# Masking the weighted values of two tiles in one VectorE instruction

## The reference, cut to what matters

```
x = x + conv(_gn(x), W)
q, k, v = qkv[0] * SCALE, qkv[1], qkv[2]          # 16 heads of 8
logits[a, b] = einsum(q, k shifted by (a, b)) + rpb[a, b]     # 49 neighbours
attn = softmax(logits)
out = sum over (a, b) of attn[a, b] * (v shifted by (a, b))
x = x + (out @ w_proj + b_proj)
```

## Time and profile before

| | |
|---|---|
| median of 3 runs | 1097.95 us (1097.91 to 1101.18) |
| profiled execution | 1098.98 us |
| its span, first to last instruction | 1097.2 us |
| mean granted TensorE clock | 0.95 |
| busy: PE, DVE, ACT, POOL | 988.8, 810.7, 642.0, 484.6 us |
| `select_heads` on DVE (L1174) | 512 instructions, 128.1 us |
| attention, 32 chunks | from about 260 us to 1065 us |

### The profile page before, as it was taken

How to read it: one execution, slowest core, us unless ns; L and a number is a source line. 1 busy time by engine, 2 the same in 40 slices (tenths; PEclk the granted TensorE clock), 3 DMA queues, 4 the chain that set the end, 5 groups by cost and what they waited for, 6 DMA issues and landing times.

```text
span 1097.2 us, 41269 instructions
## 1 busy us (share of the span) xinstructions
PE 988.8 (90%) x16485; PEld 684.8 (62%) x16485; DVE 810.7 (74%) x2111; ACT 642.0 (59%) x1808; POOL 484.6 (44%) x839
## 2 busy tenths in 40 slices
PE   4999999998999989899998999898999999999882
PEld 3666665564676666666676666666666666666651
DVE  3387774544888787879888888978798788878760
ACT  2111124003786868587877767785868677777561
POOL 5000103203654646374646556474756464555530
PEclk9999999998999989899999999998999899999895
DMA  9321002234467555555746576655657375646311
GB/s 254 91 89 45 31 16 104 92 87 147 131 159 212 150 162 157 161 164 152 218 119 196 145 206 168 166 165 161 173 138 221 95 214 136 204 114 195 97 48 57
DMA packets 122582, 154.73 MB, mean 141 GB/s; under 512 B 30832, under 2 KB 107024, under 8 KB 119064
## 3 DMA queue, kind: packets, MB, share of 16 engines
q1 hardware_dynamic: 121112, 148.20, 48.1%
q0 software_dynamic: 992, 3.90, 1.2%
q10 hardware_dynamic: 288, 0.00, 0.0%
HBM read 84.05 MB, written 67.60 MB: 138 GB/s over the span
## 4 chain that ended last, share of the span: by engine, by line
PE 68%; DVE 10%; ACT 9%; issue 8%; DMA 3%; ACTq 1%; SPq 1%; POOL 0%; POOLq 0%; DVEq 0%
PE PS L1313 16%; PE PS L1380 13%; PE PS L1419 10%; PE PS L1403 8%; PE PS L1325 6%; PE PS L1396 6%; PE PS L1362 5%; ACT area L805 3%; DVE area L1142 3%; DVE S L1163 3%; ACT S L897 3%; DVE masked L1174 2%; PE PS L1342 2%; DMA bqkv<-b_qkv 2%; PE PS L1429 1%
## 5 line engine op out<-in xcount | busy, mean ns | idle before, releaser
L687 POOL TENSOR_TENSOR late<-masked 128x48 f32<-128x48 f32 (+1 forms) x512 | 153.3, 300 | 368.3 <-DVE masked L1174 356.1
L897 ACT ACTIVATE S<-S 128x384 f32<-128x384 f32 (+1 forms) x512 | 283.0, 555 | 24.1 <-DVE S L1163 21.1
L1163 DVE TENSOR_TENSOR S<-PS,bias 128x384 f32<-128x384 f32 (+1 forms) x512 | 282.5, 552 | 2.9 <-PE PS L1380 0.2
L1380 PE MATMUL PS<-area 97*128 97x48 bf16 (+1 forms) x4096 | 249.9, 207 | 36.4 <-DVE S L1163 32.8
L1153 DVE TENSOR_REDUCE mcol<-PS 128x6 bf16<-128x480 f32 (+2 forms) x288 | 176.1, 612 | 124.5 <-PE PS L1403 124.4
L890 ACT ACTIVATE VT<-PS 128x128 f32<-128x128 f32 x448 | 132.5, 296 | 183.5 <-PE PS L1362 179.5
L1380 PEld LDWEIGHTS PS<-area 97*128 97x128 bf16 x4096 | 178.6, 102 | 83.1 <-DVE S L1163 41.3
L1419 PE MATMUL PS<-S,VT 128*18 128x48 f32 x8192 | 196.4, 214 | 12.1 <-issue 11.5
L1313 PE MATMUL PS<-padded,wconv 128*128 128x392 f32 x576 | 204.2, 503 | 3.3 <-DVE wconv L1199 3.3
L1419 PEld LDWEIGHTS PS<-S,VT 128*18 128x18 f32 x8192 | 117.1, 99 | 135.3 <-issue 69.5
L1403 PEld LDWEIGHTS PS<-area 128*128 128x128 bf16 x1568 | 144.9, 156 | 22.2 <-issue 7.4
(11 more groups left out here) (86 smaller groups left out, 921.4 us busy)
## 6 DMA issues: line engine op xcount, KB each, us to landing
area<-k_parts SPq DMA_DIRECT2D x32, 1008.0 KB, 7.1
area<-q_parts SPq DMA_DIRECT2D x64, 294.0 KB, 8.2
k_parts<-area SPq DMA_DIRECT2D x32, 504.0 KB, 8.1
k_parts<-area SPq DMA_DIRECT2D x32, 336.0 KB, 3.0
q_parts<-area SPq DMA_DIRECT2D x32, 294.0 KB, 6.7
late<-x_mid SPq DMA_DIRECT2D x18, 392.0 KB, 4.9
out<-area SPq DMA_DIRECT2D x18, 392.0 KB, 4.1
den<-sums SPq DMA_DIRECT2D x132, 49.0 KB
```

The source lines that it names most:

```text
L687: nc.gpsimd.tensor_tensor(sel[:, c % SEL_RING, :, :, t0:t0 + count], m[:, :, 0], m[:, :, 1], ALU.add).then_inc(s["summed"], 1)
L897: nc.scalar.activation(S[:, n % 4, 0:cols], S[:, n % 4, 0:cols], ACT.Exp).then_inc(s["probs"], 1)
L1163: nc.vector.tensor_tensor(S[:, n % 4, 0:cols], PS[:, SCORE + n % 2, 0:cols], bias[:, at:at + cols], ALU.add).then_inc(s["biased"], 1)
L1380: last = mm(PS[:, SCORE + n % 2, cols * g:cols * (g + 1)], key_rows[a][0:PEAK_ROW + 1, g, key:key + 128], query_rows[a][0:PEAK_ROW + 1, :, ...
```

## The change

`masked` grows from 2 x 128 to 2 x 256 columns and PE puts the weighted values of tiles 2P and 2P + 1 side by side into one bank, SUM + P % 2. `select_heads` is called in odd steps only, for the pair of tiles n - 3 and n - 2, and does one instruction over both (two where the tiles have different numbers of patches, tiles 14 and 15). It waits until both tiles are weighted. `weigh` of a tile of pair P waits until pair P - 2 is selected. POOL's instructions and their order stay as they are, but tile 2P is now signalled by the instruction that also signals tile 2P + 1.

```diff
+        def pair_offset(c, n):
+            return GROUPS * PATCH * tile_of(c % 2, n - 1)[1] // 2 if n % 2 else 0
...
-                m = masked[:, n % 2, 0:4 * q].rearrange("p (g h a t) -> p g h a t", g=2, h=GROUP_HEADS, a=PATCH)
+                first = pair_offset(c, n)
+                m = masked[:, T // 2 % 2, first:first + 4 * q].rearrange("p (g h a t) -> p g h a t", g=2, h=GROUP_HEADS, a=PATCH)
...
-                wait(dve, "weighted", T + 1)
-                wait(dve, "summed", T - 1)
...
+                pair = (TILES * c + n) // 2
+                wait(dve, "weighted", 2 * pair + 2)
+                if pair > 1:
+                    wait(dve, "summed", 2 * (pair - 1))
+                at, cols = 0, [GROUPS * PATCH * tile_of(c % 2, m)[1] // 2 for m in (n, n + 1)]
+                for size, tiles in [(2 * cols[0], 2)] if cols[0] == cols[1] else [(cols[0], 1), (cols[1], 1)]:
+                    src, to = (p.rearrange("p (g h q) -> p g h q", g=2 * tiles, h=GROUP_HEADS) for p in (
+                        PS[:, SUM + pair % 2, at:at + size], masked[:, pair % 2, at:at + size]))
+                    mask = cst[:, C_OUT:C_OUT + GROUP_HEADS].unsqueeze(1).unsqueeze(3).broadcast_to(list(src.shape))
+                    nc.vector.tensor_tensor(to, src, mask, ALU.mult).then_inc(s["selected"], tiles)
+                    at += size
...
-                    if n > 1 or c:
-                        select_heads(*next_tile(c, n, -2))
+                    if n % 2 and (n > 1 or c):
+                        select_heads(*next_tile(c, n, -3))
...
-                wait(pe, "selected", T - 1)
+                pair, first = T // 2, pair_offset(c, n)
+                if pair > 1:
+                    wait(pe, "selected", 2 * (pair - 1))
```

More of the change, by code:

```diff
@@ L255, in build @@
         mcol = sb("mcol", [128, PATCHES], BF16)
-        masked = sb("masked", [128, 2, 128])
+        masked = sb("masked", [128, 2, 256])
         halves = sb("halves", [128, 2, 128])
@@ L1166, in select_heads @@
             def select_heads(c, n):
-                q = PATCH * tile_of(c % 2, n)[1]
-                T = TILES * c + n
-                wait(dve, "weighted", T + 1)
-                wait(dve, "summed", T - 1)
-                src = PS[:, SUM + n % 2, 0:4 * q].rearrange("p (g h q) -> p g h q", g=2, h=GROUP_HEADS)
-                mask = cst[:, C_OUT:C_OUT + GROUP_HEADS].unsqueeze(1).unsqueeze(3).broadcast_to([128, 2, GROUP_HEADS, q])
-                nc.vector.tensor_tensor(masked[:, n % 2, 0:4 * q].rearrange("p (g h q) -> p g h q", g=2, h=GROUP_HEADS), src, mask,
-                                        ALU.mult).then_inc(s["selected"], 1)
+                pair = (TILES * c + n) // 2
[9 more added lines that the diff above has]
+                    at += size
             def invert(c):
@@ L1261, in _ @@
                         divide(c)
-            for n in range(TILES - 2, TILES):
-                select_heads(CHUNKS - 1, n)
+            select_heads(CHUNKS - 1, TILES - 2)
             divide(2 * IMAGES)
@@ L1415, in weigh @@
                     wait(pe, "value_out", w + 1)
-                wait(pe, "selected", T - 1)
+                pair, first = T // 2, pair_offset(c, n)
+                if pair > 1:
+                    wait(pe, "selected", 2 * (pair - 1))
                 for g in range(GROUPS):
-                    at = q * (g // 4)
-                    last = mm(PS[32 * (g % 4):32 * (g % 4) + VALUE_COLS, SUM + n % 2, at:at + q], VT[:, w % 4, g, :],
+                    at = first + q * (g // 4)
+                    last = mm(PS[32 * (g % 4):32 * (g % 4) + VALUE_COLS, SUM + pair % 2, at:at + q], VT[:, w % 4, g, :],
                               S[:, n % 4, q * g:q * (g + 1)], start=True, stop=True)
```

## The result

The changed kernel took 1125.95 us (median of 4 runs, 1124.85 to 1128.57) and the kernel before, in runs beside it, 1097.93. The ratio is 1.0263, with a 95% interval from 1.0236 to 1.0290. The forecast was 1117 us and the range ended at 1124: the sign was right, the size was not. The profiled execution took 1128.57 us, with a span of 1126.0, so 29.6 us more than the profiled one of before (1098.98).

What follows compares the result with a forecast made beforehand. The prediction took PE to bound the kernel (68% of the chain), with DVE setting the pace at the end of even chunks. Its terms, 10.5 + 8 + 0.3 = +19 us on 1097.95, gave 1117 us, range 1095 to 1124.

Steps and rivals of the forecast that it cites:

- Part 1: DVE's masked product at the end of even chunks: over a pair it occupies 0.26 us, saving 0.37 us per even chunk.
- Part 2: End of even chunks: POOL's bunched subtractions hold DVE's spreads, PE waits 0.70 us longer, 15 times, +10.5 us.
- Part 3: Odd chunks: POOL's pieces of Qbd start later, the first held by divide; PE waits about 0.6 us, +8 us in all.
- Part 4: Small effects: POOL's last two adds at the very end run one behind the other, +0.3 us; later stores count 0.
- Sum: Whole kernel: 10.5 + 8 + 0.3 = +19 us on the median of 1097.95, giving 1117 us.
- slower still: Rival: later stores and loads, or PE's longer idle times bringing more low clock, give 1125 us and over; chance 0.08.

Runs made afterwards that it cites:

- e9: Changed kernel with e8's POOL order, POOL's second subtraction cut to 8 columns from the second image on, so output incomplete: ratio 0.9702.
- e10: Kernel before, one product per tile, with e8's POOL order and POOL's second subtraction cut to 8 columns from the second image on: ratio 0.9757.
- e1: Kernel before, single products, but POOL waits until both tiles of a pair are selected and masked has four places: 1120.36 us.
- e4: Changed kernel, POOL's order in even steps made subtraction (from step 8), piece of Qbd, then add: 1094.27 us.
- e5: Kernel before, one product per tile, with the POOL order of e4: ratio 0.9980.
- e2: Changed kernel, but in even steps of odd chunks POOL writes its piece of Qbd before adding the heads: 1104.88 us.
- e6: Changed kernel plus two unused 480-column matmuls on PE ahead of the scores in steps 12 to 16: ratio 1.0156.
- e12: e8 with the extra PE matmuls of e6 in steps 12 to 16: 1086.81 us.
- e8: e4 with the last two first-kind subtractions (L711) in step 6 ahead of its add, and the first L724 behind step 8's add: 1080.38 us.

## Why the prediction was right in sign and wrong in size

**Part 1** was right about the instruction. In the timeline the product over a pair occupies 659.84 - 659.58 = 0.26 us, the value taken, and e9 against e10 has -0.35 us per even chunk, forecast -0.37. As a saving by itself it is seen only there: after has longer chunks than e1, and e4 a longer even chunk than e5.

**Part 2** was right in mechanism and size: +0.74 us in an even chunk at the upper clock, forecast +0.70, so 15 x 0.74 = 11.1 us, forecast 10.5. Both holds that it rests on are in the rows: the second spread of step 10, and the first of step 16 behind POOL's second subtraction. The steps between agree as well, counted from the start of the chunk: DVE is 0.48 us late at the end of step 10's spreads (forecast 0.44), 0.46 at the reciprocal of step 14 (0.40), 0.55 at the end of step 15's spreads (0.51). e1 shows the loss without the longer product.

**Part 3** was right in mechanism, a little small. The last piece ends 1.60 us later where 1.38 was worked out, and PE follows it by 0.26 us, where I had carried over the 0.05 us that PE takes after DVE. In the shortest chunks that is 1.60 - 0.75 + 0.26 = 1.1 us, not 0.65. In other chunks it was less. Three ends of before had 1.5 to 2.1 us of room, which Part 3 counted. And in 8 of the 15 chunks `divide` held a piece before the change already, which it did not count: it worked from one chunk without this hold, though the earlier trace rows show one with it. In the one such chunk of before without low clock the last piece ended 22.21 us into the chunk, and the loss is 23.38 - 22.96 = 0.42 us. One chunk with neither lost 23.38 - 23.04 = 0.34, and no run says why. So it is partly luck that the sum over 15 chunks, +10.0 us, is near the forecast of 8: too much was counted for some chunks and too little for others, and the sum also holds what low clock the odd chunks have in either kernel (62.2 and 57.0 us). e2, which moves the pieces alone, takes it back whole.

**Part 4**: the 0.3 us at the end did not appear; the part behind the last chunk is 0.5 us shorter.

**The Sum failed by a term it did not have.** 11.1 + 10.0 = 21 us are the steps as forecast, of 29. The other 8 are in the even chunks (19.3 - 11.1), and they come with 54 us more of low clock there. At 1.07 us for a spell of 6.8 us, as in the windows above, 54 us are worth 8.5, an estimate from that one pair of chunks; the even chunks' excess over the shortest says the same (13.2 - 5.2 = 8.0 us). I had weighed longer idle times of PE as 15 times 0.70 and 12 times 0.65 us and nothing else, in Parts 2 and 3 alike; that they would also bring more of the low level stood only in the rival "slower still", 1125 us and over, at a chance of 0.08, and that is the one that came. e6 shows that low clock has such a price: with the idle time filled, 11 to 12 us go while the even chunks at the upper level stay. That it is these 8 us of the even chunks rests on the windows and sums of after alone, since e6's gain lies in its odd chunks. The profiled execution of after also has the lowest mean clock of its four.

What stays open is why a spell comes in one chunk and not in the next: chunks 10 and 12 are alike up to its start, 18.39 and 18.31 us of PE in 19.1. I can count the spells but not forecast them: for e12 I expected 30 us of low clock or less, and it has 42.3.

## What to carry to other kernels

When a producer is merged so that it signals two pieces of work at once, the consumer's whole queue is moved: look at what stands behind the merged work there, which port it shares, and where its last instruction falls. Put the work with a deadline ahead of the work that now comes in bunches; that turned +2.6% into -1.8% here. And when a change makes PE wait at the end of a stage, price the waits by what they do to the clock too: here some 21 us of new waits brought 8 more.

## What the runs showed of the hardware

- POOL's two kinds of instructions treat DVE's spread differently. Beside a subtraction (two tensors in) it takes up to 1.00 us and ends 0.11 to 0.12 us behind it; only a spread that starts in the subtraction's last 0.15 us or so takes its free 0.31. A piece of `Qbd` (one tensor and a scalar) holds it in two parts of its 1.26 us and leaves it free between them. DVE and then POOL in odd chunk 9 of before, where the spread starts 0.01 us behind the piece:

```profile
517.34 0.69 DVE L1142 TENSOR_SCALAR area<-area,cst 128x392 bf16<-128x392 bf16 x1
```

```profile
517.33 1.26 POOL L727 TENSOR_SCALAR area<-area,cst 128x392 bf16<-128x392 bf16 x1
```

  And in odd chunk 13, where it starts 0.43 us behind:

```profile
615.76 0.31 DVE L1142 TENSOR_SCALAR area<-area,cst 128x392 bf16<-128x392 bf16 x1
```

```profile
615.33 1.26 POOL L727 TENSOR_SCALAR area<-area,cst 128x392 bf16<-128x392 bf16 x1
```

  In before, after, e2 and e8 a spread that starts up to 0.36 us behind a piece of 1.26 us ends 0.70 us behind the piece's start; one that starts 0.42 to 0.59 us behind it takes 0.31 to 0.32 us; one that starts 0.74 to 1.02 us behind it ends 0.11 to 0.12 us behind the piece. `divide` holds L727 (1.98 to 2.08 us instead of 1.26) when it starts 0.2 us ahead of it. The Trainium skill, in "SBUF — State Buffer", section "Who interferes with whom", has an instruction of VectorE in a 2-port mode and one of GpSimd exclude each other for the whole instruction; that holds for the subtractions, and for L727 only in its two parts. By the same section VectorE's instructions with two inputs in SBUF, as `divide`, contend with GpSimd's that read SBUF. The trace agrees where `divide` comes first; where L727 of before came 0.65 to 0.82 us ahead of it, both took their free times (1.26 and 0.97 us).
- PE starts 0.25 to 0.26 us behind the recorded end of POOL's instruction that releases it, at all 15 places in after, and 0.06 us behind DVE's, at the ends of the 15 even chunks.
- Low clock in an already waiting stretch cost about a sixth of its length (1.07 us of 6.8), since PE's slower work fills its own idle time. Other even chunks of after with 6.8 us of it took 0.97 to 1.66 us more than the shortest, and odd ones 2.9 to 3.8 us more.
